# State-space mixer rearranged: 64x64 products on both halves of the partitions, in three runs per octet

## The reference, cut to what matters

```python
# per channel d (256 of them) and state n (64), over t = 0..1023, for each of 4 sequences
u  = layernorm(layernorm(x)) * ln_gamma + ln_beta
dA = exp(-exp(log_A) * dt[:, None]);  dB = B_param * dt[:, None]
h  = dA * h + dB * u[..., None]
y  = einsum('dn,bdn->bd', C_param, h) + D_param * u
x  = x + layernorm(x) + einsum('btd,ed->bte', y, W_out) + b_out
```

## Time and profile before

| | us |
|---|---|
| median of 3 runs (range) | 1049.09 (1048.56 to 1052.2) |
| the profiled execution's own time | 1048.15 |
| its span, first to last instruction | 1046.4 |
| TensorE busy in the span | 916.5 |
| VectorE busy | 576.4 |
| ScalarE busy | 532.0 |
| GpSimd busy | 206.2 |

### The profile page before, as it was taken

How to read it: one execution, slowest core, us unless ns; L and a number is a source line. 1 busy time by engine, 2 the same in 40 slices (tenths; PEclk the granted TensorE clock), 3 DMA queues, 4 the chain that set the end, 5 groups by cost and what they waited for, 6 DMA issues and landing times.

```text
span 1046.4 us, 15287 instructions
## 1 busy us (share of the span) xinstructions
PE 916.5 (88%) x5059; PEld 726.4 (69%) x5059; DVE 576.4 (55%) x948; ACT 532.0 (51%) x784; POOL 206.2 (20%) x239
## 2 busy tenths in 40 slices
PE   3200998976999999999999999999999999999996
PEld 0000988854778777877787778777877877787885
DVE  6598886663555555545454654555455555453421
ACT  2356675231665366446635663575366536645431
POOL 2365364100400130022003100400040014002000
PEclk9999999995999999999999999999999999999999
DMA  8984332134000200010001001100100020001000
GB/s 256 340 324 142 106 110 77 61 120 187 1 1 1 86 0 0 20 65 0 0 35 50 0 0 45 40 0 0 53 32 0 0 85 0 0 20 41 1 1 22
DMA packets 13502, 60.70 MB, mean 58 GB/s; under 512 B 2579, under 2 KB 4246, under 8 KB 12598
## 3 DMA queue, kind: packets, MB, share of 16 engines
q1 hardware_dynamic: 13382, 60.32, 16.8%
q10 hardware_dynamic: 64, 0.07, 0.0%
q0 software_dynamic: 32, 0.00, 0.0%
HBM read 46.09 MB, written 23.72 MB: 67 GB/s over the span
## 4 chain that ended last, share of the span: by engine, by line
PE 71%; DVE 12%; issue 9%; ACT 4%; DMA 2%; POOL 1%; DVEq 1%; POOLq 0%; ACTq 0%; SPq 0%
PE pair L1050 43%; PE pair L1037 9%; PE pair L1009 3%; PE pair L998 3%; PE pair L469 2%; PE pair L1025 2%; PE pair L461 2%; PE pair L509 2%; PE pair L975 1%; PE pair L1018 1%; DMA V<-V 1%; DVE V L348 1%; DMA ring<-kernel_rows 1%; DVE vbuf L898 1%; DVE V L347 1%
## 5 line engine op out<-in xcount | busy, mean ns | idle before, releaser
L751 ACT ACTIVATE vbuf<-pair,scl 128x512 f32<-128x512 f32 x128 | 87.8, 686 | 237.2 <-PE pair L1050 231.4
L1050 PE MATMUL pair<-h1hi,h_turned 128*128 128x512 f32 x512 | 204.1, 399 | 1.5 <-DVE h1lo L869 1.5
L1050 PE MATMUL pair<-h2hi,h_turned 128*128 128x512 f32 x512 | 202.6, 396 | 0.0
L1050 PE MATMUL pair<-h1lo,h_turned 128*128 128x512 f32 x512 | 199.8, 390 | 0.0
L1050 PE MATMUL pair<-h2lo,h_turned 128*128 128x512 f32 x512 | 199.6, 390 | 0.0
L869 DVE TENSOR_TENSOR h1lo<-vbuf,h1hi 128x512 fp32r<-128x512 f32 x80 | 57.7, 721 | 119.5 <-ACT h1hi L752 118.7
L1050 PEld LDWEIGHTS pair<-h1hi,h_turned 128*128 128x128 f32 x512 | 96.1, 188 | 34.5 <-issue 10.5
L1050 PEld LDWEIGHTS pair<-h2hi,h_turned 128*128 128x128 f32 x512 | 96.1, 188 | 25.2 <-issue 5.9
L869 DVE TENSOR_TENSOR h2lo<-vbuf,h2hi 128x512 fp32r<-128x512 f32 x64 | 44.2, 690 | 123.5 <-ACT h2hi L752 123.5
L1037 PE MATMUL pair<-zThi,w_turned 128*128 128x512 f32 x256 | 105.6, 413 | 5.3 <-DVE vbuf L898 2.7
L1050 PEld LDWEIGHTS pair<-h2lo,h_turned 128*128 128x128 f32 x512 | 96.2, 188 | 19.3
(11 more groups left out here) (117 smaller groups left out, 1484.0 us busy)
## 6 DMA issues: line engine op xcount, KB each, us to landing
h_turned<-d_h SPq DMA_DIRECT2D x2, 4096.0 KB, 14.3
xres<-in_x SPq DMA_DIRECT2D x8, 512.0 KB, 7.0
ring<-alpha_rows SPq DMA_DIRECT2D x16, 256.0 KB, 3.7
ring<-kernel_rows SPq DMA_DIRECT2D x16, 256.0 KB, 3.5
x_rows<-x1t SPq DMA_DIRECT2D x8, 512.0 KB, 2.6
xr<-x_rows SPq DMA_DIRECT2D x8, 512.0 KB, 3.5
out<-xr SPq DMA_DIRECT2D x8, 512.0 KB, 2.6
x_rows<-xres SPq DMA_DIRECT2D x7, 512.0 KB, 2.6
```

The lines of the kernel that those rows point to most:

```text
L751: e.activation(vb[:, s % 2, :], h_ps[s % 4], ACT.Gelu, scale=sc)
L1050: ins = e.matmul(bank, w[:, k, m * P:(m + 1) * P], src[part][:, k, :], start=(k == 0 and part == 0), stop=(k == HC - 1 and part == 1))
```

## The change

`V` is replaced by four tensors. `tok` (128 x 64 chunks x 128 channels) has the steps of channels 0 to 127 on partitions 0 to 63 and those of channels 128 to 255 on partitions 64 to 127; it is loaded from a new host layout `xs` of x, in eight transfers, and is normalised in place. `GG` holds the carried blocks, `EE` all state weights (loaded once, 16 transfers), `scan` the scanned states in two buffers. There are 16 octets of 2 x 8 channels. Per channel pair there are now three kinds of products, all with K = 64 and M = 64: state (L459), Toeplitz (`within`, L466) and carried (L473), the last two adding up in one PSUM bank. The two channels of a pair use other rows and other columns of the array. In an octet all state products come first, then all Toeplitz products, then the carried products of the octet before.

```diff
-    V = nc.alloc_sbuf_tensor_at("V", [P, DM, BC], F32, offset=zone)
+    tok = nc.alloc_sbuf_tensor_at("tok", [P, BC, P], F32, offset=t["zone_a"])
+    GG = nc.alloc_sbuf_tensor_at("GG", [P, P, L], F32, offset=t["zone_a"] + 4 * P * BC)
+    EE = nc.alloc_sbuf_tensor_at("EE", [P, P, N], F32, offset=t["zone_b"])
...
-        e.dma_start(V[N:P, P:DM, :], V[0:N, 0:P, :]).then_inc(g_moved, 16)
-        for n in ("w1", "w2", "h1", "w3", "h2"):
-            e.dma_start(t["d" + n], a[n]).then_inc(w_d, 16)
...
+        for n in ("w1", "w2", "w3", "h1"):
+            e.dma_start(t["d" + n], a[n]).then_inc(w_d, 16)
+        for n in ("xW", "keys", "scl"):
+            e.dma_start(t[n], a[n]).then_inc(k_in, 16)
+        for g in range(NBLK):
+            e.wait_ge(h_ps, 2 * g + 2)
+            e.dma_start(xres[:, 4 * g:4 * g + 4, :], a["x"][:, 4 * g:4 * g + 4, :]).then_inc(xr_in[g], 16)
+            if g == 4:
+                e.wait_ge(w_d, 64)
+                for n in ("w1", "w2"):
+                    e.dma_start(t[n].bitcast(F32), t["d" + n]).then_inc(w_in, 16)
+        for n in ("h1", "w3"):
+            e.dma_start(t[n].bitcast(F32), t["d" + n]).then_inc(w_in, 16)
+        e.dma_start(t["dh2"], a["h2"]).then_inc(w_d, 16)
...
+        def inverse(b):
+            e.wait_ge(chain, 10 * b + 10)
+            here = slice(SB * b, SB * b + SB)
+            e.tensor_tensor(rs[:, :, here], sv[:, :, here], mhalf[:, :, :], ALU.pow).then_inc(powd, 1)
+        def gamma(g):
+            e.wait_ge(z_rdy, 8 * g + 8)
+            v = tok[:, 8 * g:8 * g + 8, :]
+            e.tensor_tensor(v, v, gam[:, :].unsqueeze(1).to_broadcast([P, 8, P]), ALU.mult).then_inc(z_g, 1)
...
+        for o in range(NOCT):
+            e.wait_ge(y_ps, o + 1)
+            e.activation(tok[:, :, OCT * o:OCT * o + OCT], yps[o % 4].rearrange("p (i c) -> p c i", i=OCT), ACT.Copy).then_inc(y_out, 1)
+            if o % 2 == 1 and o // 2 + 2 < NGRP:
+                tt_load(e, o // 2 + 2)
+            if o % 2 == 1 and o >= 5:
+                residual_base((o - 5) // 2)
...
+        for o in range(NOCT + 1):
+            if o < NOCT and o % 2 == 0:
+                e.wait_ge(t_mask, o + 2)
+            if o + 1 < NOCT and o % 2 == 1:
+                e.wait_ge(e_rdy, o // 2 + 2)
+            if o >= 1:
+                e.wait_ge(h_scan, o)
...
+            if o + 1 < NOCT:
+                for c in range(OCT):
+                    ins = state(o + 1, c)
+                ins.then_inc(h_ps, 1)
+            if o < NOCT:
+                for c in range(OCT):
+                    ins = within(o, c)
+                ins.then_inc(w_ps, 1)
+            if o >= 1:
+                e.wait_ge(w_ps, o)
+                for c in range(OCT):
+                    ins = carried(o - 1, c)
+                ins.then_inc(y_ps, 1)
```

More of the change, by code:

```diff
@@ new lines, in sync @@
+        e.wait_ge(coef, 2)
+        for u in range(2):
+            e.dma_start(alS[P * (1 - u):P * (2 - u), :], al2[:, u, :]).then_inc(al_st, 16)
+        for g in range(4, 8):
+            e.dma_start(tok[:, 8 * g:8 * g + 8, :], a["xs"][:, 8 * g:8 * g + 8, :]).then_inc(x_in[g], 16)
+        for v, dst in ((a["gamma"], gam), (a["beta"], bet)):
+            for h in range(2):
+                e.dma_start(dst[L * h:L * h + L, :], v[P * h:P * h + P].partition_broadcast(L)).then_inc(bc_in, 16)
+        e.wait_ge(al_st, 32)
@@ L163, in sync @@
         for g in range(2):
[L164 to L171, removed]
+            tt_load(e, g)
+        for n in ("w1", "w2", "w3", "h1"):
[12 more added lines that the diff above has]
+        e.dma_start(t["dh2"], a["h2"]).then_inc(w_d, 16)
     def x1_store(e, i):
@@ new lines, in bias @@
+        def bias(tile):
+            if tile == 0:
+                e.wait_ge(wo_in, 32)
+            e.wait_ge(base, tile + 1)
+            e.wait_ge(t_mask, min(2 * (tile // 4 + 5), 2 * NGRP))
+            e.tensor_tensor(xres[:, tile, :], xres[:, tile, :], bo[:, :], ALU.add).then_inc(base_b, 1)
+        for g in range(4):
+            mask(g)
+        for g in range(4, NGRP):
+            mask(g)
+            for j in range(4):
+                bias(4 * (g - 4) + j)
+        for tile in range(4 * (NGRP - 4), TILES):
+            bias(tile)
@@ new lines, in scalar @@
+        for v in range(4):
+            row_evac(v)
+        e.wait_ge(const, 9)
+        norm_apply(0)
+        entry_exp(0)
+        norm_apply(1)
+        entry_exp(1)
+        entry_exp(2)
+        norm_apply(2)
+        entry_exp(3)
+        norm_apply(3)
+        for g in range(4, NGRP):
+            entry_exp(g)
+        e.wait_ge(natural, 4)
+        for o in range(NOCT):
[5 more added lines that the diff above has]
+                residual_base((o - 5) // 2)
@@ new lines, in stats, with beta @@
+        def stats(b, steps):
+            for c in range(SB):
+                if c % 8 == 0:
+                    e.wait_ge(x_in[2 * b + c // 8], 16)
+                e.bn_stats(st4[:, b % 2, c, 0:2, :].rearrange("p a m -> p (a m)"), tok[:, SB * b + c, :]).then_inc(stat, 1)
+                if steps and c >= 4:
+                    steps.pop(0)()
+        def beta(g):
+            e.wait_ge(*((z_g, g + 1) if g < 6 else (z_h, g - 5)))
+            v = tok[:, 8 * g:8 * g + 8, :]
+            e.tensor_tensor(v, v, bet[:, :].unsqueeze(1).to_broadcast([P, 8, P]), ALU.add).then_inc(z_b, 1)
@@ new lines, in vector @@
+        stats(0, [])
+        stats(1, [lambda n=n: chain_step(0, n) for n in range(11)])
+        stats(2, [lambda n=n: chain_step(1, n) for n in range(11)])
+        e.wait_ge(bc_in, 64)
+        beta(0)
+        beta(1)
+        stats(3, [lambda n=n: chain_step(2, n) for n in range(11)])
+        e.wait_ge(k_ps, 4)
+        for row in (0, N):
+            e.tensor_copy(GG[row:row + 1, :, L - 1], edit[row:row + 1, 1, :]).then_inc(g_row, 1)
+        for n in range(10):
+            chain_step(3, n)
@@ L485, in tensor, with state @@
-        e.wait_ge(e_rdy, 1)
-        states(0, 0, (h_scan, 1))
-        turn(0, False)
-        with e.Fori(1, DM // OCT // 4 - 1) as it:
-            turn(it, False)
-        turn(DM // OCT // 4 - 1, True)
+        def state(o, c):
+            i = OCT * o + c
+            for h in range(2):
+                rhs = tok5[L * h:L * h + L, i, :, 0:CH - 1]
+                rows = slice(N * (1 - h), N * (2 - h))
+                out = hps[o % 2][rows, c * BC:(c + 1) * BC].rearrange("p (b c) -> p b c", b=BATCH)[:, :, 1:CH]
+                ins = e.matmul(out, EE[L * h:L * h + L, i, :], rhs, start=True, stop=True)
+            return ins
@@ new lines, in within, with carried @@
+        def within(o, c):
+            i = OCT * o + c
+            for h in range(2):
+                rows = slice(L * h, L * h + L)
+                ins = e.matmul(yps[o % 4][rows, c * BC:(c + 1) * BC], TT[o // 2 % 2][rows, (i % GRP) * L:(i % GRP + 1) * L], tok[rows, :, i], start=(c == 0), stop=False)
+            return ins
+        def carried(o, c):
+            i = OCT * o + c
+            for h in range(2):
+                rows, other = slice(L * h, L * h + L), slice(N * (1 - h), N * (2 - h))
+                ins = e.matmul(yps[o % 4][rows, c * BC:(c + 1) * BC], GG[other, i, :], scan[other, o % 2, c * BC:(c + 1) * BC], start=False, stop=(c == OCT - 1))
+            return ins
```

521 lines of the change are left out of this document (226 added, 295 removed).

## The result

The changed kernel takes 1055.55 us (median of 4 runs, 1054.29 to 1057.2), the kernel before 1049.38 beside it (4 runs, 1048.56 to 1052.2): ratio 1.0059, 95% interval 1.0036 to 1.0082. It is slower by 0.6%, 4.5 us above the forecast and inside the range. The profiled execution took 1054.29 us, span 1052.6, against 1046.4 before: +6.2.

A forecast was written before the change was run, and what follows sets the result against it. Taken as bounding: normalisation's chain of steps, TensorE's pace in the octet loop, a chain of small steps in the tail. Terms -18.6 + 12.9 + 8.3 = +2.6 us gave 1051 us; 80% range 1036 to 1068.

The forecast's parts named there:

- Rival 2: Normalisation: a power call costs 1.67 us whatever its size, saving 15.6 us; 1036 us in all, chance 0.12.
- 10 L + 6 C: Octet loop: 16 octets plus six waits for the Toeplitz mask, 34 + 44.4 = 78.4 us before extras.
- L: Octet loop: time for one octet's 24 product pairs, 3.4 us, with bounds 2.8 and 4.4.
- C: Octet loop: chain from Toeplitz load issue through two masks to the first product, 7.4 us.
- Cold start and clock: Octet loop: 1.7 us for slow first records plus 5 us for lower granted clock behind the waits.
- The shared load: Octet loop: Toeplitz load sharing the DMA engines with `w1` and `w2`, 1.5 us extra.
- Rival 6: Octet loop: a pair's two products run one after the other, octet 6.7 us; 1079 us in all, chance 0.11.
- Rival 3: Octet loop: no stride penalty (-6 us) and the clock stays up in waits (-5); 1040 us, chance 0.13.
- Rivals 4: Octet loop: strided moving reads take twice the time, octet 4.4 us; 1058 us in all, chance 0.12.
- rival 5: Octet loop: TensorE stays at the low clock throughout, octet 5.1 us; 1061 us in all, chance 0.08.
- T: End of the octet loop, its last evacuation, from which tail times count; forecast at 171.3 us.
- the cover: Tail: the wait for queued `vblk`, landing near T + 23, hides `residual_base` calls that would otherwise cost 4 us.

The follow-up runs named there:

- experiment 7: Changed kernel with GpSimd raising only 16 elements a batch to the power, VectorE deriving the second scales by formula: 1049.65 us, ratio 1.0005 to the kernel before.
- experiment 3: Changed kernel with state and Toeplitz products reading contiguous `GG` instead of strided `tok` (output not the layer's): 1053.86 us, ratio 1.0045 to the kernel before.
- experiment 4: Changed kernel with all four weight loads and the copy of h2 issued ahead of the loop: 1050.86 us, ratio 1.0009 to the kernel before.
- Experiments 1: Changed kernel with the DRAM copy of h2 issued behind `vblk` and `xbo` instead of ahead of them: 1052.65 us, ratio 1.0024 to the kernel before.
- experiment 5: Changed kernel with each group of residual activations on ScalarE two groups earlier in the loop, queue unchanged: 1058.73 us, ratio 1.0091 to the kernel before.

## Why the prediction was right, step by step

The sign of the sum and the places of loss were as forecast; the spans give -17.5 in front, +17.9 in the loop and +5.9 behind it, where -18.6, +12.9 and +8.3 had been forecast. The total is as near as it is because the loop's miss of 5.0 and the tail's of 2.4 have opposite signs.

**Normalisation: right in the number**, 85.10 against 84, **with some luck.** The power of 32 elements took 5.42 to 5.46 us three times and 6.33 once, against 5.6; gamma 2.34 against 2.4. Rival 2, a power of flat price, falls: 16 elements take 3.13, 32 take 5.66. I had charged 5 us for VectorE beside the masks. The larger delay was one I had no row for, VectorE beside GpSimd's gamma (experiment 7): in the changed kernel `ng` of L380 took 2.32 us behind three of the four powers. The last gamma ended at 77.2 instead of 72.7, so 4.5 us were lost before the masks began, and beside them one beta took 2.05 us instead of 1.23. The 5 us stood in the wrong place and covered a delay that I had not listed. How the 17.5 us gained divide between beta, gamma and the move within SBUF that is gone, no run shows.

**The loop: right in mechanism, 5.0 us too low in size.** With the forecast's 10 L + 6 C:
- L was 3.55 against 3.4, so 10 L is 1.5 more. The two halves of that miss have opposite signs. Without a stride the pairs are quicker than the 2.8 that I took (2.4 to 2.5 for the products of an octet), and the stride costs 1.0 to 1.1 us an octet, where transposes with strided weights had suggested 0.6. The Trainium skill, page "SBUF — State Buffer", section "Door 1: The DMA port swizzle", has each access that crosses to a new 16-byte line pay; experiment 3 agrees for the moving side, with those 1.0 to 1.1 us at the upper clock.
- Cold start and clock together cost 5.4 us against 6.7; the low clock cost less than my 1.7 us an octet, as it does not slow the strided products (experiment 3): outside C the products took 40.9 us (11.8 up to the start at 96.92, 21.9 for five iterations of 4.1 to 4.5 behind the waits, 7.2 from 169.34 to the last product at 176.53), less 35.5.
- C, from the load's issue to the first product, was 6.6 to 7.3 us in five groups against 7.4, and 11.7 in the one whose load shared the engines. Their sum is 46.2 against 45.9 (6 x 7.4 + 1.5). The shared load was mis-sized (+4.7 by experiment 4 instead of +1.5), and the other five hid it by being 0.5 lower each.
- **The term that was missing:** the load is issued after the *evacuation* of the odd octet, not at the end of its products. From the start of the next iteration to the load's issue it took 0.70 to 0.77 us, six times: 4.4 us. My C began with the load, my iteration ended with the products, and this lay between.

So 1.5 - 1.3 + 0.3 + 4.4 and 0.2 for the last evacuation give 5.1, the 5.0 within rounding.

**Rival 6 falls.** Products of a pair one after the other would have made an octet 6.7 us; it was 3.55, and 2.4 to 2.5 with contiguous data. That is 198 records in 7.36 us, 37 ns from one to the next, and 27 in experiment 3, where 8 products one after the other had 59. The Trainium skill, page "TensorEngine Tiling (Array Packing)", section "Restrictions and Gotchas", says that different row tiles cannot access the same PSUM bank at the same time. The trace does not agree for tiles that write different partitions of one bank: two such 64x64 tiles, straight or crossed, ran side by side here. **Rival 3** falls: the clock fell behind every wait, and the stride had its price, so neither of its gains came. Nor are the two independent: without the stride the low clock costs more (experiment 3). **Rivals 4 and 5** fall: L was 3.55 and not 4.4, and the iteration behind the slow one had a granted clock of 0.84 to 1.00. The 5.1 us of rival 5 for an octet at the lower level, for which no row was given, is too high: at 0.50 it took 4.5.

**The tail: right as a sum, with one path mis-sized.** The transposes came at T + 26.1 (forecast 26.5), GpSimd could clear `vblk` at T + 22.8 (landing forecast at T + 23). The forecast's own terms, 23 + 0.5 + 1.0 + 1.4, make 25.9 and not 26.5; the steps took 3.2 us instead of 2.9. Of the 8.4 us lost until then, 2.5 are regained by the end of the span, where I had counted 0.5. The trace bears out part of that: eight transposes of `tok` take 1.04 to 1.09 us instead of 1.33; where the rest comes from was not traced. The step that is wrong is the size of the path under the cover, with TensorE at the transposes by T + 22. `residual_base` was hidden as forecast, but by 1.4 us only: the third projection ended at T + 24.7. Experiments 1 and 4 took the cover away, and the transposes stood at T + 24.4 and T + 24.3. I had let ScalarE's 6 us run beside TensorE's turns and not asked what the 5.7 us of idle time do to the first projection: 5.7 us instead of 3.6. The cost without cover is 6.8 us (24.4 - 17.6), not 4: 3.9 for the eight activations more that stand ahead, 0.9 for eight transposes at the low clock and 2.0 for the projection.

## What to carry to other kernels

Issue a refill when the last reader of the buffer is done, not in the engine list behind the evacuation that follows. And count the iterations between the release and the need: one iteration of 3.55 us against a chain of about 7 is a wait each time, and a quicker iteration (experiment 3) mostly lengthens it: 5.7 us more waiting, 3.6 us less time.

If a stage's end has two waits that run in parallel, trying each alone shows little or even a loss; take both away in one kernel before judging either. A small transfer on which a chain hangs goes ahead of the megabytes in its queue.

## What the runs showed of the hardware

- After idle stretches of 3.6 to 4.2 us the granted clock of the next iteration was 0.50 to 0.60, near the lower of the two levels (1.2 of 2.4 GHz), and cost 0.5 to 0.9 us (4.1 to 4.5 against 3.6); with 8.7 us idle ahead it was 0.52 in the loop (4.39 us) and 0.69 in the tail of experiment 5. So a wait costs more than its length, and where in a chain it lies matters: experiment 5 removed one wait, made a later one longer, and lost 3.2 us.
- The strided Toeplitz products took 1.29 us for 20 records at a granted clock of 0.50 and at 1.00. A low clock cost the contiguous iteration 1.6 us and the strided one 0.8.
- A moving fp32 operand whose elements lie 512 bytes apart made 16 pairs of 60- and 64-column products slower by 1.0 to 1.1 us at the upper clock, 62 to 71 ns a pair.
- GpSimd's power costs about 0.16 us an element of a partition over the whole span seen: 1.02 us for 4, 1.67 for 8, 2.91 (undisturbed) for 16, 5.43 for 32.
- A VectorE operation of 16 or 32 elements that starts with a GpSimd gamma of 1024 elements ends with it: 2.3 us, where one of 32 elements with nothing beside it took 0.19.
